# A triangle multiplication taken by pairs of channels, and the operand loads and stores around the last projection block reordered

## The reference, cut to what matters

```python
ab1, ab2, ab3 = (gate_proj(zn, Wg_i, bg_i, W_i, b_i) * zm for i in 1, 2, 3)    # 192 x 192 x 64 each
pp = gate_proj(_ln(protein_pair), Wg2, bg2, W2, b2)
lp = gate_proj(_ln(l_pair), Wg1, bg1, W1, b1)
ip = gate_proj(_ln(inter_pair), Wg1, bg1, W1, b1)
block = einsum('bikc,bkjc->bijc', pp, ab1) + einsum('bikc,bjkc->bijc', ab2, lp) + ab3 * ip
out = sigmoid(zn @ Wend + bend) * (_ln(block) @ Wsum + bsum) * zm
x = x + out          # then layer norm, routed experts, layer norm, residual
```

## Time and profile before

| | |
|---|---|
| Runs of the kernel, median (lowest to highest) | 1469.97 us (1468.67 to 1471.53), 3 runs |
| The profiled execution | 1468.26 us |
| Its span, first to last instruction | 1466.4 us |
| Mean granted TensorE clock | 0.972 of full speed |
| Busy shares: TensorE, VectorE, ScalarE, GpSimd | 93%, 84%, 67%, 69% |
| Projection phase | from the start to about 574 us |
| Triangle phase | about 575 to 721.5 us |
| Mix phase begins | 721.8 us |
| Moved by DMA | 270.6 MB, 185 GB/s over the span |

### The profile page before, as it was taken

One profiled execution on the slowest core, in us unless ns is written; L12 is line 12 of the kernel. 1 busy time (PEld: TensorE's weight loads), 2 busy tenths in 40 slices (PEclk: granted clock), 3 DMA queues, 4 the chain that ended last, 5 costly groups with the idle time before them and its releaser, 6 DMA issues. The chain is left out here.

```text
span 1466.4 us, 32189 instructions
## 1 busy us (share of the span) xinstructions
PE 1363.1 (93%) x9880; PEld 1135.3 (77%) x9880; DVE 1228.7 (84%) x4156; ACT 984.5 (67%) x2293; POOL 1012.6 (69%) x1557
## 2 busy tenths in 40 slices
PE   5999999999999986999789999699999999999993
PEld 2877778877788865878666666599999999999983
DVE  6998999899899963777699999677888888888996
ACT  3888888888888864334267777355776766767763
POOL 3999999999999984444378888444555555555663
PEclk9999999999999997999899999699999999999997
DMA  9999999999999978999789996311222222232222
GB/s 213 208 261 245 262 246 253 237 254 256 248 243 247 259 193 256 292 283 291 187 242 296 301 300 202 106 44 54 76 77 71 84 76 83 72 87 73 73 58 72
DMA packets 358394, 270.63 MB, mean 185 GB/s; under 512 B 60720, under 2 KB 333074, under 8 KB 358226
## 3 DMA queue, kind: packets, MB, share of 16 engines
q1 hardware_dynamic: 356528, 267.90, 69.6%
q10 hardware_dynamic: 1426, 0.46, 0.2%
q0 software_dynamic: 272, 0.21, 0.1%
HBM read 174.17 MB, written 94.37 MB: 183 GB/s over the span
## 5 line engine op out<-in xcount | busy, mean ns | idle before, releaser
L1498 ACT ACTIVATE hT<-psH_d,b 128x512 f32<-128x512 f32 x288 | 197.9, 689 | 158.4 <-PE psH_d L1538 158.3
L642 PE MATMUL psZ_a<-w_all,xT_a 128*128 128x128 f32 x1728 | 231.3, 277 | 5.0 <-DVE low_pp L717 5.0
L642 PE MATMUL psZ_a<-w_all,xT_block 128*128 128x384 f32 x576 | 213.8, 494 | 8.9 <-DVE low_ab L711 5.7
L642 PEld LDWEIGHTS psZ_a<-w_all,xT_a 128*128 128x128 f32 x1728 | 211.0, 193 | 7.8 <-issue 5.2
L566 ACT ACTIVATE sig_a<-psZ_a 128x256 f32<-128x256 f32 (+1 forms) x360 | 153.7, 427 | 87.1 <-PE psZ_a L642 49.0
L578 POOL TENSOR_SCALAR shared<-shared,coefs_early 128x128 f32<-128x128 f32 x468 | 204.9, 460 | 0.0
L629 PE MATMUL psT_a<-ident,shared 128*128 128x128 f32 x1152 | 186.5, 274 | 3.6 <-issue 2.1
L629 PEld LDWEIGHTS psT_a<-ident,shared 128*128 128x128 f32 x1152 | 141.5, 142 | 54.5 <-issue 27.2
L1565 POOL TENSOR_TENSOR u_d<-u_d,gamma 128x512 f32<-128x512 f32 x72 | 96.1, 1335 | 124.1 <-ACT u_d L1481 108.9
L1192 DVE TENSOR_SCALAR shared<-shared,coef 128x128 f32<-128x128 f32 x288 | 179.2, 681 | 1.6 <-POOL xh_b L1572 1.6
L1572 POOL TENSOR_TENSOR xh_b<-shared,b 128x512 f32<-128x512 f32 x72 | 93.3, 1296 | 105.3 <-DVE ffn_sum L1633 104.1
(11 more groups left out here) (224 smaller groups left out, 3175.5 us busy)
## 6 DMA issues: line engine op xcount, KB each, us to landing
shared<-in_x_dram SPq DMA_DIRECT2D x48, 512.0 KB, 5.7
scratch_xT<-xT_block SPq DMA_DIRECT2D x36, 512.0 KB, 5.2
shared<-scratch_xT SPq DMA_DIRECT2D x36, 512.0 KB, 4.9
scratch_x<-x_c SPq DMA_DIRECT2D x36, 512.0 KB, 4.1
shared<-scratch_x SPq DMA_DIRECT2D x36, 512.0 KB, 3.5
shared<-in_x_dram SPq DMA_DIRECT2D x48, 256.0 KB, 5.3
shared<-L_conv_protein_pair_dram SPq DMA_DIRECT2D x24, 512.0 KB, 7.5
shared<-in_L_conv_l_pair_dram SPq DMA_DIRECT2D x24, 512.0 KB, 9.2
```

The source lines that it names most:

```text
L642: ins = nc.tensor.matmul(out, turned_x(G, i, t0, size)[:, j * P:j * P + P], rhs[i], start=True, stop=True)
L1498: nc.scalar.activation(hT[:, S % 2, f, :], psH[:, f, :], ACT.Gelu, bias=s["b1"][:, f:f + 1]).then_inc(gelued, 1)
```

## The change

In the last block of the projection phase SyncE's order is written anew (`last_body`). In the x pass each third of xT is stored when it is turned, and the pp and lp outputs of the block before behind the first and second third; the first operands' early columns are loaded after that. After the three operand-and-store steps of the x, pp and lp passes come the late columns, each set behind the stores it depends on; sta_high is loaded when three groups of the ip pass are turned (`STA_GROUPS`), in front of the last wait. In the triangle phase TensorE takes a pair of channels at a time: three wide products of the first channel, the next pair's transpositions, three wide products of the second, then the narrow products of both. The other engines' code is the same.

```diff
@@ -387,6 +387,7 @@
 
 
 N_LOADS = 9
+STA_GROUPS = -(-OPERAND // (PASSES[3][2] * CH))
 
 
 def project_phase(nc, d, s):
@@ -487,39 +488,50 @@
                 for k in range(len(CHUNKS)):
                     load_third(i, k, 0)
 
-            def body(n, last):
+            def body(n):
                 for i in range(len(PASSES)):
-                    if not last:
-                        for k in range(len(CHUNKS)):
-
-                            sp.wait_ge(turned, NG_A * n + PASS_START[i] + CHUNKS[k][1] // PASSES[i][2])
-                            load_third(i, k, n + 1)
-                            if i == 0:
-                                store_xT(n, k)
-                                if n > 0 and k < 2:
-                                    store_out(n - 1, k + 1)
-                    else:
-
-                        sp.wait_ge(turned, NG_A * n + PASS_END[i])
-                        sp.wait_ge(stored[min(i, 2)], 48 * n)
-                        load_operands(OPERANDS[2 * i:2 * i + 2], 0, N - BLOCK_A)
+                    for k in range(len(CHUNKS)):
+
+                        sp.wait_ge(turned, NG_A * n + PASS_START[i] + CHUNKS[k][1] // PASSES[i][2])
+                        load_third(i, k, n + 1)
                         if i == 0:
-                            for k in range(len(CHUNKS)):
-                                store_xT(n, k)
-                                if k < 2:
-                                    store_out(n - 1, k + 1)
-                        if last and i > 0:
-                            store_out(n, i)
+                            store_xT(n, k)
+                            if n > 0 and k < 2:
+                                store_out(n - 1, k + 1)
                     if i == 0:
                         store_out(n, 0)
-            for n in range(NBLK):
-                body(n, n == NBLK - 1)
+
+            def last_body(n):
+
+                early, late = (0, N - BLOCK_A), (N - BLOCK_A, N)
+                of_ab, of_pp, of_lp = (("ab1_high", "ab1_low", "ab2_low"), ("pp_low", "mov_high"), ("lp_low",))
+                for k in range(len(CHUNKS)):
+                    sp.wait_ge(turned, NG_A * n + PASS_START[0] + CHUNKS[k][1] // PASSES[0][2])
+                    store_xT(n, k)
+                    if k < 2:
+                        store_out(n - 1, k + 1)
+                sp.wait_ge(stored[0], 48 * n)
+                load_operands(OPERANDS[0:2], *early)
+                store_out(n, 0)
+                for i in range(1, 3):
+                    sp.wait_ge(turned, NG_A * n + PASS_END[i])
+                    sp.wait_ge(stored[i], 48 * n)
+                    load_operands(OPERANDS[2 * i:2 * i + 2], *early)
+                    store_out(n, i)
+                sp.wait_ge(stored[0], 48 * NBLK)
+                load_operands(of_ab, *late)
+                sp.wait_ge(stored[1], 48 * NBLK)
+                load_operands(of_pp, *late)
+                sp.wait_ge(turned, NG_A * n + PASS_START[3] + STA_GROUPS)
+                load_operands(OPERANDS[6:], *early)
+                sp.wait_ge(stored[2], 48 * NBLK)
+                load_operands(of_lp + OPERANDS[6:], *late)
+
+            for n in range(NBLK - 1):
+                body(n)
+            last_body(NBLK - 1)
             for k in range(len(CHUNKS)):
                 sp.wait_ge(stored_xT[k], 16 * NBLK)
-            for i in range(3):
-                sp.wait_ge(stored[i], 48 * NBLK)
-            load_operands(OPERANDS, N - BLOCK_A, N)
-
 
         def norm(wait, engine_op, sem_out, n, G, which, last):
 
@@ -812,6 +824,10 @@
                     load_turned(sp, d, s, p, k)
                     load_tiles(sp, mix_buffers(s)[0][:, p], d["x"], p, s["loaded_x"][p][k], ch)
 
+        def high_half(mov, h):
+
+            return mov.rearrange("p (n u) -> p n u", u=LOW)[:, :, HIGH * h:HIGH * h + HIGH]
+
         @block.tensor
         def _(pe):
             ident = s["ident"]
@@ -831,27 +847,30 @@
                     ins = nc.tensor.transpose(ends(half), row(par, "ab1_high", a, 2 * q), ident[:])
                 ins.then_inc(turned, 1)
 
+            def sides(Q, e):
+
+                return [(sta[:, Q % 2, e, :], mov[:, Q % 2, e, :]) for sta, mov in ((ab1T, pp_now), (lp_now, ab2_now), (sta_now, mov_now))]
+
             turn(0)
-            for C in range(HID):
-                Q, e = divmod(C, 2)
-                if e == 0:
-                    pe.wait_ge(copied, Q + 1)
-                    pe.wait_ge(packed_act, Q + 1)
-                    pe.wait_ge(packed_pool, Q + 1)
-                    pe.wait_ge(packed_dve, Q + 1)
-                need(pe, taken, 2 * (C - 3))
-                out = psO[:, C % 4, :]
-                steps = [(sta[:, Q % 2, e, :], mov[:, Q % 2, e, :]) for sta, mov in ((ab1T, pp_now), (lp_now, ab2_now), (sta_now, mov_now))]
-                for k, (sta, mov) in enumerate(steps):
-                    nc.tensor.matmul(out[:, 0:N], sta[:, 0:P], mov, start=(k == 0), stop=(k == 2))
-                for k, (sta, mov) in enumerate(steps):
-                    for h in range(2):
-                        part = mov.rearrange("p (n u) -> p n u", u=LOW)[:, :, HIGH * h:HIGH * h + HIGH]
-                        ins = nc.tensor.matmul(out[64 * h:64 * h + 64, N:N + N // 2], sta[:, P:N], part,
-                                               start=(k == 0), stop=(k == 2))
-                ins.then_inc(summed, 1)
-                if e == 0 and Q + 1 < PAIRS_B:
-                    turn(Q + 1)
+            for Q in range(PAIRS_B):
+                pe.wait_ge(copied, Q + 1)
+                pe.wait_ge(packed_act, Q + 1)
+                pe.wait_ge(packed_pool, Q + 1)
+                pe.wait_ge(packed_dve, Q + 1)
+                for e in range(2):
+                    C = 2 * Q + e
+                    need(pe, taken, 2 * (C - 3))
+                    for k, (sta, mov) in enumerate(sides(Q, e)):
+                        nc.tensor.matmul(psO[:, C % 4, 0:N], sta[:, 0:P], mov, start=(k == 0), stop=(k == 2))
+                    if e == 0 and Q + 1 < PAIRS_B:
+                        turn(Q + 1)
+                for e in range(2):
+                    C = 2 * Q + e
+                    for k, (sta, mov) in enumerate(sides(Q, e)):
+                        for h in range(2):
+                            ins = nc.tensor.matmul(psO[64 * h:64 * h + 64, C % 4, N:N + N // 2], sta[:, P:N], high_half(mov, h),
+                                                   start=(k == 0), stop=(k == 2))
+                    ins.then_inc(summed, 1)
 
         @block.scalar
         def _(act):
```

## The result

| | before | after |
|---|---|---|
| Median (lowest to highest), 5 runs each, taken together | 1471.53 us (1468.67 to 1474.14) | 1462.12 us (1461.04 to 1466.10) |
| Ratio, 95% interval | | 0.9939 [0.9923, 0.9955] |
| Profiled execution, its span | 1468.26, 1466.4 us | 1466.10, 1464.2 us |

The change brings 9 us; 12.4 were forecast. The profiled execution of after is the longest of its five. Its triangle phase ends 4.35 us earlier than before's, and what comes behind it took 747.0 us against 744.9. That code is the same in both, and over the fourteen profiles of all kernels here but those with half loads, two queues or earlier issue it scatters from 742.9 to 747.5, so nothing is read from it.

A forecast was written before the change was run, and what follows sets the result against it. DMA was taken to set the hand-over and, slightly ahead of TensorE, the triangle phase. 10.4 + 1.2 + 0.85 = 12.4 us off 1468.26 gives 1455.9, the median 1.7 higher; forecast 1457, range 1450 to 1462.5.

The forecast's parts named there:

- Hand-over, -10.4: Projection to triangle phase: earlier stores let the second group's first issue, and all behind it, come 10.4 us earlier.
- Pair of 3.94, nearly none of it kept: Triangle phase: TensorE's pair takes 3.94 instead of 4.30 us, 11.5 us over 32 pairs, nearly all lost waiting for loads.
- DMA gives way: Rival, triangle phase: loads issued earlier come at TensorE's pace, 16.2 us per group, total 1449 us; chance 0.08.
- Lead, -1.2: Triangle phase: next loads issued 4.3 us ahead of a landing instead of 3.5, saving 1.2 us, bounds 0 and 3.
- the clock falls at the gates: Rival, triangle phase: TensorE's idling lowers its clock, 2.3 us per fall, 18.2 per group, total 1462 us; chance 0.04.
- Tail, -0.85: Triangle phase's end: last add comes 19.35 us behind the last landing instead of 20.2, keeping 0.85 us.
- The rival on VectorE: Triangle phase: VectorE's adds and packing become the bound, slower, about 1478 us at 4.9 us per pair; chance 0.02.

The follow-up runs named there:

- half loads: Kernel before, then changed kernel, loading only half of each operand's columns from the third group on: 1469.4 us (0.9972) and 1446.91 us (0.9815).
- two queues: Changed kernel, then kernel before, with the second 64-partition transfers of ab1_high and mov_high issued from ScalarE's queue: 1466.44 us (0.9966) and 1475.68 us (1.0014).
- earlier issue: Mixed kernel, then changed kernel, each operand loaded again once its own reader is through, operand order changed too: 1470.26 us (0.9997) and 1472.93 us (1.0013).
- hand-over alone: Kernel before with only the new last block, TensorE's old order in the triangle phase: 1459.68 us (0.9915); later 1460.59 and 1459.36 us.
- later issue alone: Changed kernel with SyncE waiting for one more pair's sums before issuing a group's loads: 1467.86 us, ratio 0.9965 to before.
- filled gates: Changed kernel with the first channel's wide products repeated ahead of gated transpositions: once 1460.93 us (0.9921), twice 1461.78 (0.9924) and 1461.57 us (0.9920).
- mixed kernel: New last block, TensorE's old order in the first seven groups and its new order in the last group only: 1459.57 us, ratio 0.9917 to before.
- pair order alone: Kernel before with only TensorE's new order by pairs in the triangle phase, old last block: 1473.17 us, ratio 1.0014.

## Why the prediction was right in part

- **Hand-over, -10.4: right.** Measured alone it brings 11.4, 10.6 and 12.3 us (medians on three chips; by the ratios 12.5, 11.8 and 10.0). Each step shows: no wait of VectorE, 1.33 us transpositions, projections ended at 557.5 for 558, last confirmation at 561.60 for "561 to 562", second group issued at 563.95 for 563.9. One term was too small: from the confirmation to the first transposition it takes 4.7 us, not 3.1 (three loads in 1.7 us of issue, then the landing), hence 566.26 instead of 564.5 (565.0 to 567.0 in the other profiles with the whole hand-over). In the profiles the last addition comes 9.1 to 9.6 us earlier with the hand-over alone. The medians show 1 to 3 us more than that; the profiled execution of before, at 1468.26, had run about 3 us under the medians of before on those chips (1471.09 to 1471.65).
- **Pair of 3.94, nearly none of it kept: right.** 3.95, and 11.1 us when the loads are halved. "DMA gives way" is out: intervals were longer with the new order, not 16.2.
- **Lead, -1.2: this step failed.** The step took a group's packing to end 13.1 us behind its landing, so that the lead grows from 3.5 to 4.3 us, and held that a longer lead can only bring the landings closer. Both parts fail. The next issue comes 13.8 us behind an undisturbed gate, after 14.0 before. The forecast's own terms give 13.6 (0.66 + 1.07 + 1.13 for the rest of the pair, two pairs of 3.94, and packing until 2.9 behind them). The mean lead from the second group on is 3.9 us (four profiles with the new order) against 3.6 (six with the old). And the intervals grew: 17.77 became 18.31 us on average, so that six of them lose 3.3 us instead of gaining 1.2.
- **What the lead does is known only in part.** Over 98 intervals in 14 profiles the mean is 19.9 us behind leads under 2 us, 18.5 for 2 to 3, 18.0 for 3 to 4, 17.4 above 4. That isn't its price: the issue follows the landing ahead by about 14 us, so a lead is long because the interval ahead of it was long. Those intervals average 20.0 us and 5.7 MB ahead of leads above 5 us, and 17.1 us and 4.5 MB ahead of leads under 2. Long and short take turns, as bytes of the next group move in the one and are missing in the other. What points to a price is the later issue alone: 1.8 us in the triangle phase, 3.5 to 6.6 in the whole time, the first from one profile of each and the second with intervals that overlap.
- **What stands in its place.** Part of it is shown: with the new order TensorE waits at 20 of 28 gates, 0.4 to 5.1 us and 1.7 on average; behind nine of them the clock is at half, and the next issue comes 15.2 to 16.4 us behind such a gate instead of 13.8. This is the forecast's rival "the clock falls at the gates", given 0.04, with its 2.3 us per fall (1.4 to 2.6 measured as delay of the issue). It was weighed by one wait of 1.43 us that left the clock alone, and the waits were taken to be alike, 1.6 to 2. The rival's 18.2 us per group and 1462 us are close to what was measured, but it had a fall at every gate, so that is in part luck. With filled gates the intervals are 17.87 to 17.95. Taken from the second landing to the eighth, the new order moves 272 to 283 GB/s, the old 283 to 293 and the filled 289 to 291, at busy shares of 0.94 to 0.97, 0.95 to 0.97 and 0.96 to 0.98. So only the smaller part of the loss is idle time of the DMA engines; for the most part a busy microsecond moves less (GB/s over share: 289 to 294 against 293 to 302). Why it does is not shown.
- **Tail, -0.85: right in size.** 19.3 to 20.0 us with the new order where the clock held at the last gate; 20.9 in after, where it fell. The terms of the forecast for it add up to 18.9, not to the 19.35 that it gives; where the other 0.45 comes from isn't said.
- **Balance.** The pair order was worth -2.05 in the forecast. Alone it measures +2.1 [-0.1, +4.3]; in the changed kernel +1.4 and +1.9 against the hand-over alone on the same chips. -11.4 and +2 give the 9 us. That the sign is plus rests on three comparisons of one direction, each within its own uncertainty. 1462.12 lies just inside the 1450 to 1462.5 of the forecast. That is partly luck, as the hand-over brought 1 us more than its term and the pairs 4 less than theirs.
- **One more slip.** The rival on VectorE would by its own threshold (no gain at 4.73 us per pair) end at about 1475 us for 4.9, not at 1478.

The Trainium skill, page "TensorE: Matmul & The Clock Gate", part 1, has the clock halved behind a long enough idle stretch. The runs agree in so far as the half clock stands behind waits, of 5.06 us and, in the same profile, of 1.84. But 2.71 in another left the clock at 1.00, so the length of the wait alone doesn't decide here.

## What to carry to other kernels

Time spared on an engine whose phase is paced by loads may be worth less than nothing: it becomes idle time in front of the gates, the clock can fall there, and what is late behind it is the next issue. Spare it only where no gate follows (the last group), and look first at the hand-over, where stores in front of the loads behind them brought 9 us for a few lines. When a queue has work issued group by group, read the lead of each issue over the landing ahead of it, and the bytes moved in each interval with it: a short interval behind a long one can be the same work counted in the other. An issue later by 1.2 us went with a triangle phase 1.8 us longer here.

The best versions run are the hand-over alone and the mixed kernel (0.9915 to 0.9932, and 0.9917). The hand-over alone is 1.4 and 1.9 us under the changed kernel on the same chips, within the uncertainty; the mixed kernel was not run beside it.

## What the hardware showed unexpectedly

- With the DMA engines full, the 64-partition transfers move 178 to 264 GB/s and the 128-partition ones about 415, from one queue and from two. The Trainium skill, page "SBUF — State Buffer", sections "Door 1: The DMA port swizzle (why `[64,N]` ≈ `[32,N]`)" and "Can I just issue two DMAs to hit both halves?", says that 64 partitions at one end reach half the ports and that a second transfer beside the first adds 6%. The windows agree in the main: side by side they moved 246 to 264 GB/s (605 to 608 us), far from 422, though one behind the other, in the third profile of the changed kernel (604 to 607 us), it was 203 to 234, so more than 6% may be gained.
- A wait's length alone does not tell whether the clock falls: 1.84 us did it in after, 2.71 (658.46 us, second profile of the changed kernel) and 2.97 (671.33, pair order alone) did not.
- A group's landing lags behind the end of full traffic: shares of 0.21 and 0.09 from 601 to 603 us for a landing at 605.06 (first kernel with earlier issue), 0.27 and 0.13 from 636 to 638 for one at 639.32 (second profile of the changed kernel).
- In after one interval was 21.14 us although its transfers were issued 3.04 ahead. The DMA engines were full throughout and moved 6.07 MB, 0.96 more than the group has; the next group, issued 7.38 us ahead of the landing, shared them. Whether an early issue delays the group in flight was not tested by itself.
